# A routed expert stage: last weights loaded raw per tile, eight row buffers, and transposes moved among the down products

## What is computed

```python
def reference(x, src, dst, ...):
    x = x + _L0_gnn_ref(_layernorm(x), edge_index, rms_w, W_down, Wl, Wr, att, W_up)
    x = x + _L0_ffn_ref(_layernorm(x)[None], expert_tokens, W1, b1, W2, b2, W3, b3)[0]
    return x

# _L0_ffn_ref: 8 experts, each token goes to the 2 best
def _expert_mlp(x, W1, b1, W2, b2, W3, b3):
    h = gelu(x @ W1 + b1)      # 1024 -> 64
    h = gelu(h @ W2 + b2)      # 64 -> 64
    return h @ W3 + b3         # 64 -> 1024
```

## Time and profile before

| | |
|---|---|
| median of 3 runs | 2009.55 us (2003.25 to 2011.63) |
| profiled execution | 2005.56 us, its span 2003.6 us |
| granted PE clock over the span | 0.93 |
| PE, PEld busy | 1642.9, 1321.5 us |
| DVE, ACT, POOL busy | 1299.5, 772.3, 783.6 us |
| DMA | 311.76 MB, mean 156 GB/s |
| group loop | about 787 to 1180 us |
| tile loop | 1203 to 1997 us |

### The profile page before, as it was taken

How to read it: one execution, slowest core, us unless ns; L and a number is a source line. 1 busy time by engine, 2 the same in 40 slices (tenths; PEclk the granted TensorE clock), 3 DMA queues, 4 the chain that set the end, 5 groups by cost and what they waited for, 6 DMA issues and landing times.

```text
span 2003.6 us, 27936 instructions
## 1 busy us (share of the span) xinstructions
PE 1642.9 (82%) x8625; PEld 1321.5 (66%) x8625; DVE 1299.5 (65%) x2446; ACT 772.3 (39%) x1342; POOL 783.6 (39%) x758
## 2 busy tenths in 40 slices
PE   3999999999676573999899947888887888787886
PEld 2788888888532242877777736666666666666665
DVE  4655555555255663976788755677777777677776
ACT  3444444444132260000200005555555555555553
POOL 2211111112188402555476542444444444444443
PEclk9899999999898795988888878999999999999999
DMA  9244444441544324899998864666656666556421
GB/s 239 77 129 131 132 127 130 128 125 44 139 121 109 117 89 134 198 253 245 239 243 240 232 198 124 169 176 184 192 161 177 178 174 171 158 170 174 115 48 35
DMA packets 128365, 311.76 MB, mean 156 GB/s; under 512 B 69455, under 2 KB 75981, under 8 KB 116651
## 3 DMA queue, kind: packets, MB, share of 16 engines
q1 hardware_dynamic: 58809, 181.56, 35.9%
q0 software_dynamic: 66208, 108.34, 18.3%
q10 hardware_dynamic: 3234, 20.48, 3.3%
HBM read 188.85 MB, written 138.85 MB: 164 GB/s over the span
## 4 chain that ended last, share of the span: by engine, by line
PE 47%; DMA 19%; DVE 12%; issue 7%; ACT 6%; POOL 5%; SPq 3%; DVEq 0%; POOLq 0%; ACTq 0%
DMA rows_x<-cx 13%; PE psum L1533 12%; PE psum L1535 10%; PE psum L1534 10%; DVE xt_lo L1450 5%; DVE xb L1469 4%; PE psum L1558 4%; PE psum L1551 3%; PE psum L1814 2%; POOL xls L617 2%; PE psum L1845 2%; ACT xt_hi L857 2%; POOL td L621 2%; ACT gl L871 1%; DMA xb<-rows_x,idx_in 1%
## 5 line engine op out<-in xcount | busy, mean ns | idle before, releaser
L1533 PE MATMUL psum<-xt_hi,st_w 128*128 128x256 f32 x528 | 178.3, 338 | 142.0 <-DVE xt_lo L1450 140.4
L698 POOL DMA_INDIRECT out<-xb,idx_in x132 | 184.3, 1397 | 149.7 <-DVE xb L1469 118.2
L857 ACT ACTIVATE xt_hi<-psum 128x512 fp32r<-128x512 f32 x264 | 150.7, 596 | 224.3 <-PE psum L1814 206.4
L1450 DVE TENSOR_TENSOR xt_lo<-psum,xt_hi 128x512 fp32r<-128x512 f32 x264 | 175.6, 683 | 87.0 <-ACT xt_hi L857 72.5
L1533 PEld LDWEIGHTS psum<-xt_hi,st_w 128*128 128x128 f32 x528 | 102.6, 194 | 186.1 <-DVE xt_lo L1450 182.8
L851 ACT ACTIVATE xn<-xb 128x1024 f32<-128x1024 f32 x132 | 156.3, 1231 | 58.3 <-DMA xb<-rows_x,idx_in 58.2
L961 DVE TENSOR_TENSOR axt_lo<-psum,axt_hi 128x500 fp32r<-128x500 f32 x160 | 108.5, 678 | 108.1 <-ACT axt_hi L730 94.4
L689 POOL DMA_INDIRECT xb<-rows_x,idx_in x132 | 140.7, 1066 | 86.0 <-POOL xb L685 54.0
L1814 PE MATMUL psum<-ident,xn 128*128 128x128 f32 x1056 | 152.6, 279 | 25.9 <-ACT xn L851 25.6
L1469 DVE SCALAR_TENSOR_TENSOR xb<-psum,xb 128x512 f32<-128x512 f32 x264 | 169.3, 682 | 1.0 <-PE psum L1535 0.8
L829 ACT ACTIVATE aggt_hi<-psum 128x500 fp32r<-128x500 f32 x40 | 21.5, 585 | 378.0 <-PE psum L1730 335.5
(11 more groups left out here) (280 smaller groups left out, 4388.6 us busy)
## 6 DMA issues: line engine op xcount, KB each, us to landing
rows_x<-cx SPq DMA_DIRECT2D x20, 1806.0 KB
cx<-in_x SPq DMA_DIRECT2D x20, 1792.0 KB
ax<-in_x SPq DMA_DIRECT2D x19, 1792.0 KB
st_half<-experts SPq DMA_DIRECT2D x66, 512.0 KB
node_table<-trow ACTq DMA_DIRECT2D x19, 896.0 KB
node_table<-xld SPq DMA_DIRECT2D x10, 500.0 KB
st_half<-experts SPq DMA_DIRECT2D x66, 64.0 KB
rows_x<-cx SPq DMA_DIRECT2D x20, 209.6 KB
```

The costliest lines, as they stand in the source:

```text
L698: pool.indirect_dma_start(out=out[:, :], out_offset=bass.IndirectOffsetOnAxis(ap=idx_in[:, t % NI, s:s + 1], axis=0), in_=xb[:, b, s, 0:D] ...
L857: act.activation(xt_hi[:, 2 * q:2 * q + 2, :].rearrange("p k n -> p (k n)"), T_R[q % 2], ACT.Copy).then_inc(r_hi, 1)
L1450: dve.tensor_tensor(xt_lo[:, 2 * q:2 * q + 2, :].rearrange("p k n -> p (k n)"), T_R[q % 2], xt_hi[:, 2 * q:2 * q + 2, :].rearrange("p k n ...
L1533: pe.matmul(out_ap, left[0], right[0], start=start, stop=False, skip_group_check=True)
```

## The change

Six things, in the tile loop and in what feeds it:

1. W3 is no longer kept as a table. SP loads it raw per tile from HBM (`load_w3`, both experts, 2 x 256 KB) into one of N3 = 3 buffers; ACT makes the high part (`upper_w3`, 128x1024) and POOL the low part (`lower_w3`). The DVE copy of 64x2048 and the DMA within SBUF of 512 KB go.
2. W2 keeps a table of 7 slots, without its zero blocks: 2 loads in the group loop, one split on ACT, one on POOL; the copies per tile go to a quarter of `st_w2`, whose zeros are set once.
3. Eight row buffers instead of four, and gathers five tiles ahead instead of two (`AHEAD = 5`, sixteen index buffers). The clear of the extra columns moves into `put_rows`.
4. PE: the transposes of quarters 0 and 1 of tile t+1 move from behind the last down product to before `hidden2`; quarters 2 and 3 stand one step earlier, ahead of `hidden1(t, 0)` and `hidden1(t, 1)`.
5. ACT: `norm_r(t + 1)` comes before `gelu_1`, the first two `high_r` of t+1 before `gelu_2`, and `upper_w3(t + 1)` last. DVE: both `stage_w1` ahead of `low_1`; `lower_w2` and the first two `low_r` of t+1 ahead of `low_2`.
6. Between the stages, ACT, DVE and SP wait for all stores of rows_x1, since the new buffers lie over those of the group loop; DVE then clears `st_w2` and four row buffers (128 x 8256).

```diff
-NX, NI = 4, 8
+NX, NI, AHEAD = 8, 16, 5
+NOLD, NR, N3 = 4, 4, 3
...
@@ SP, group loop
-                if 0 <= g - 1 < SLOTS:
-                    load_half(g - 1)
+                if g == 1:
+                    for a in range(2):
+                        sp.dma_start(w2_raw[EH * a:EH * (a + 1), :, EH:2 * EH],
+                                     w2[a:a + SLOTS].rearrange("e h k -> h e k")).then_inc(raw_w2, 16)
...
@@ SP, tile loop
-            def upper_w3(t):
-                slot = sp.value_load(tile_tab[0:1, 2, t:t + 1], min_val=0, max_val=SLOTS - 1)
-                wait(sp, r_y, 4 * (t - 1))
-                wait(sp, w3_up, 16 * t)
-                sp.dma_start(st_half[EH:2 * EH, t % 2, 0:2 * D].bitcast(F32),
-                             experts[EH:2 * EH, bass.ds(slot, 1), 0:2 * D].rearrange("p a b -> p (a b)").bitcast(F32)
-                             ).then_inc(w3_up, 16)
+            def load_w3(t):
+                for a in range(2):
+                    slot = sp.value_load(tile_tab[0:1, 1 + a, t:t + 1], min_val=0, max_val=SLOTS - 1)
+                    if a == 0:
+                        wait(sp, r_w3lo, t - N3 + 1)
+                        wait(sp, w3_in, 32 * t)
+                    sp.dma_start(w3_raw[EH * a:EH * (a + 1), t % N3, :],
+                                 w3[bass.ds(slot + a, 1), :, :].rearrange("e h n -> (e h) n")).then_inc(w3_in, 16)
...
-            load_list(0)
-            load_list(1)
-            sp.wait_ge(half_lo, 2 * SLOTS)
-            sp.wait_ge(x1_put[0], 32 * ((NG + 2) // 3))
-            upper_w2(0)
-            upper_w3(0)
-            load_list(2)
-            load_list(3)
+            for t in range(AHEAD):
+                load_list(t)
+            for b in range(3):
+                sp.wait_ge(x1_put[b], 32 * ((NG - b + 2) // 3))
+            load_w3(0)
+            load_w3(1)
+            sp.wait_ge(w2_lo, 1)
+            sp.wait_ge(cleared, 3)
+            upper_w2(0)
+            load_w3(2)
+            load_list(AHEAD)
+            load_list(AHEAD + 1)
             for t in range(NT):
                 if t + 1 < NT:
                     upper_w2(t + 1)
-                if t >= 1:
-                    upper_w3(t)
-                if t + 4 < NT:
-                    load_list(t + 4)
+                if t + N3 < NT:
+                    load_w3(t + N3)
+                if t + AHEAD + 2 < NT:
+                    load_list(t + AHEAD + 2)
...
@@ POOL
             def take_rows(t):
-                b = t % NX
-                wait(pool, rows_out[b], 32 * (t // NX))
-                pool.memset(xb[:, b, :, D:D + 2], 0.0).then_inc(r_clear, 1)
+                b = t % NR
+                if t >= NX:
+                    pool.wait_ge(rows_out[(t - NX) % NR], 32 * ((t - NX) // NR + 1))
...
+            def lower_w3(t):
+                pool.wait_ge(r_w3hi, t + 1)
+                pool.tensor_tensor(st_w3[:, t % N3, 1, :], w3_raw[:, t % N3, :], st_w3[:, t % N3, 0, :].bitcast(F32),
+                                   ALU.subtract).then_inc(r_w3lo, 1)
...
             for t in range(NT):
-                if t + 2 < NT:
-                    take_rows(t + 2)
+                if t + AHEAD < NT:
+                    take_rows(t + AHEAD)
+                if t >= 1:
+                    lower_w3(t)
                 if t >= 1:
                     put_rows(t - 1)
...
@@ ACT
+            def upper_w3(t):
+                act.wait_ge(w3_in, 32 * (t + 1))
+                wait(act, r_y, 4 * (t - N3 + 1))
+                act.activation(st_w3[:, t % N3, 0, :], w3_raw[:, t % N3, :], ACT.Copy).then_inc(r_w3hi, 1)
...
             for t in range(NT):
-                pair = pair_of(t)
                 high_r(t, 2)
                 high_r(t, 3)
+                if t + 1 < NT:
+                    norm_r(t + 1)
+                pair = pair_of(t)
                 gelu_1(t, pair)
                 if t + 1 < NT:
-                    norm_r(t + 1)
+                    high_r(t + 1, 0)
+                    high_r(t + 1, 1)
                 gelu_2(t, pair)
                 choose(t, pair)
                 if t + 1 < NT:
-                    high_r(t + 1, 0)
-                    high_r(t + 1, 1)
+                    upper_w3(t + 1)
...
@@ DVE
+            dve.memset(st_w2[:, :, :, :].bitcast(F32), 0.0).then_inc(cleared, 1)
+            dve.memset(xb[:, NOLD:NX, :, :], 0.0).then_inc(cleared, 1)
...
                     stage_w1(t + 1, 0, e)
+                    stage_w1(t + 1, 1, second_of(t + 1))
                 low_1(t)
-                if more:
-                    stage_w1(t + 1, 1, second_of(t + 1))
                 if t >= 1:
                     result(t - 1, 0)
                     result(t - 1, 1)
+                if more:
+                    lower_w2(t + 1, e)
+                    low_r(t + 1, 0)
+                    low_r(t + 1, 1)
                 low_2(t)
                 if t >= 1:
                     result(t - 1, 2)
                     result(t - 1, 3)
-                if more:
-                    lower_w2(t + 1, e)
-                    low_r(t + 1, 0)
-                    low_r(t + 1, 1)
-                    lower_w3(t + 1, e)
...
@@ PE
             for t in range(NT):
+                turn_r(t, 2)
                 hidden1(t, 0)
-                turn_r(t, 2)
+                turn_r(t, 3)
                 hidden1(t, 1)
-                turn_r(t, 3)
                 hidden1(t, 2)
                 hidden1(t, 3)
                 if t >= 1:
                     down(t - 1, 0)
                     down(t - 1, 1)
+                if t + 1 < NT:
+                    turn_r(t + 1, 0)
+                    turn_r(t + 1, 1)
                 hidden2(t)
                 if t >= 1:
                     down(t - 1, 2)
                     down(t - 1, 3)
-                if t + 1 < NT:
-                    turn_r(t + 1, 0)
-                    turn_r(t + 1, 1)
```

156 lines of the change are left out of this document (80 added, 76 removed).

## The result

| | before | after |
|---|---|---|
| median of the runs compared, us | 2006.51 (4 runs) | 1906.63 (4 runs, 1898.59 to 1920.06) |
| ratio to before, 95% interval | | 0.9512 (0.9476 to 0.9549) |
| profiled execution, us | 2005.6 | 1920.06 |
| its span, us | 2003.6 | 1918.2 |

What follows compares the result with a forecast made beforehand. A ring of waits bounds the tile loop, PE waiting for xt_lo; after the change POOL at 9.4 us a step. Terms -15 - 143 + 4 = -154 give 1851 profiled, 1855 against the median, range 1815 to 1946.

Steps and rivals of the forecast that it cites:

- Group loop, -15: Stage before the tile loop: 14 weight loads of 256 KB leave it, saving 15 us.
- Between the stages, +4: Start of the tile loop: W3's first load lands later, +4 us (0 to +8); DVE's memset hidden under the first gather.
- PE allows 8.9: Tile loop: with the wait for xt_lo gone, PE's own issue time permits a step of 8.9 us.
- POOL needs 9.4: Tile loop: POOL's work, stretched 1.4 by DVE copies, sums to 9.4 us a step (8.9 to 9.8), the longest; -143 us.
- rival 2: Tile loop: POOL's subtraction holds a DVE instruction on the ring of waits; step 10.6 us, total 1933, chance 0.25.
- The lock: Tile loop: a DVE copy meeting POOL's subtraction may wait up to 2.4 us; cost 0 to 2.4 a step, taken as 0.
- Then POOL falls behind and the meeting is over: Objection to rival 2: in the tile loop the low part would come first by a hair, at about 6.9 us.
- Rivals 1, 3 and 4: Tile loop alternatives: PE bound, 1823, chance 0.20; W3 late, 2080, 0.04; step stays 11.5, 1992, 0.03.
- Rival 1: Tile loop: DVE's copies fall into POOL's gaps, nothing is held, PE is the bound; total 1823, chance 0.20.
- rival 3: Tile loop: W3's loads arrive late, over 32 us; at 35 us a step of 13, total 2080, chance 0.04.

Runs made afterwards that it cites:

- e6: Only the new loop order of PE, ACT and DVE put into the kernel before; old weight table, four buffers, gathers two ahead stay: 2012.90 us, ratio 1.0056.
- e4: The changed kernel with the zeros of the four new row buffers written by ACT instead of DVE's memset: 1875.97 us in one profiled execution.
- e1: The changed kernel plus the gate: POOL waits for hidden 2's low part before its W3 subtraction. 1804.87 us, ratio 0.9009.
- e12: e1 with one more small instruction on ACT at the start, zeros still on DVE: 1805.59 us, ratio 0.9021.
- e3: The changed kernel with POOL's W3 subtraction done twice, same result: 1916.48 us, ratio 0.9564.
- e11: The kernel of e4 once more (zeros on ACT, no gate), timed in rounds: 1894.15 us, ratio 0.9486.
- e10: The changed kernel with the gate of e1 and the zeros on ACT: 1845.59 us, ratio 0.9256.
- e2: The changed kernel with POOL's W3 subtraction cut to 64 of 1024 columns from the fourth tile on: 1806.33 us, ratio 0.9008.

## Why the prediction was right and wrong

- **Group loop, -15: right in kind, a little large.** The seven groups from the second start to the ninth last 151.2 us before and 139.4 after. e6, which keeps the old loads, has 148.4 for them. The change and the eleven other kernels with raw weights run have 135.9 to 141.5, mean 138.6. So the loads are worth (151.2 + 148.4) / 2 - 138.6 = 11 us. When the group loop begins differs by some 10 us between kernels that are alike up to there, so the 11.2 us at the first normalization say little by themselves.
- **Between the stages, +4 with the memset "under that gather": the cover was wrong.** The memset held the first gather (6.06 instead of 1.06, by e4). It cost little: ACT waited 2.02 us for these rows behind W3's high part. In e4, without the hold, W3's first load was the later one and the loop began no sooner.
- **PE allows 8.9: right.** e1 runs at 8.95 and e12 at 8.96 a step, PE full.
- **POOL needs 9.4: wrong, and this is the step that carried the forecast.** The sum is 8.06 (e3). 8.0 without disturbance was right; the 1.4 for stretched scatters and gathers was taken from rows where a 1.21 us copy L1490, which the change removes, or a w1 copy lay on a gather, and I let all three copies fall on one each. One stretch of 0.46 is what e3 shows. POOL waited 105.5 of 500 us for DVE's results in the change, so it was never the bound. That 1907 lies inside the stated range owes nothing to this step: the range was drawn to take in rival 2.
- **The lock, "between 0 and 2.4 a step; I take 0": wrong.** The step is 10.71 - 8.95 = 1.8 us longer than in e1, 114 us in the loop. Of this the pairs with and without the gate give the lock 0.9 (e11, e10) to 1.1 (e4, e1), 57 to 71 us. The rest is the difference between traces with and without PE's late signals, which no term of the prediction had: where they come the loop is slower with the gate (9.62 for 8.95), and without it more steps hold the w2 copy (23 in the change, 19 in e11, 3 in e4). The places were nearly right: the subtraction starts 6.4 us after the last result (1461.75 against 1454.11 + 1.27), and I had 6.5 to 7.5. But the w2 copy, which I put at 5.5, stands at 6.0 (1461.42): where I had "a microsecond or more" between them there are 0.3 us, and by the rows even a copy that starts those 0.3 us first is held.
- **Rival 2, 10.6 a step: right, and its objection was not.** The mean is 10.71, made of steps of 10.06 with the second low part held (0.14 below the lower end that the rival gave) and of 11.2 to 11.5 with the copy or the first low part held, which its sum did not price. "Then POOL falls behind and the meeting is over" fails because POOL waits for DVE's fourth result in each step. The hold delays DVE, DVE delays the clear, and the clear moves the subtraction along with what it meets. So the meeting renews itself, and 63 of 65 steps have one. Its total of 1933 is 26 too slow, for two reasons in the main. It counts from the undisturbed step of 11.60 where the mean was 11.90, so that it leaves 65 x 0.3 = 19.5 us of start-up and late gathers in, which went with the early gathers. And the profiled execution of before lies 4 us below its median, that of after 13 above. Some 10 us go the other way: 10.71 is 7 us more in the loop than 10.6, and the tail is 3 us longer. That its number is near is in part luck, since the late signals, which it didn't have, lie in the measured time: e4, which has none and differs from the change in who writes the zeros, took 1875.97 in its one execution.
- **Rivals 1, 3 and 4.** Rival 1 (PE is the bound, 1823) is what e1, e2 and e12 are, at 1805 with those late gathers gone too. ACT never waited for W3 in the loop, so rival 3 does not occur. (Its sum also leaves out the 11 us that the group loop and the start give: 35 us loads would be 2070.)

The sums close. For the profiled execution 1851 was forecast and 1920 came: 69 us. The tail gives 3 of them, the start none. The loop gives 66: the lock taken at nothing, with the late signals, 65 x (10.71 - 8.95) = 114, less POOL's sum put above PE's 65 x (9.40 - 8.95) = 29, less the late gathers not credited 19.5. The medians are 52 apart instead of 69 by the 4 and 13 us just named.
